# Two global attentions: heads in row and column groups of TensorE, scores computed twice, a pipeline of eight tasks

## The reference

```
gx = groupnorm(x)
xn = layernorm_channels(gx) * gamma1 + beta1
q, k, v = xn @ w_qkv + b_qkv                     # layer 0
o  = softmax(q k^T / 4) v                        # each head, 512 x 512
x1 = layernorm(o) * gamma2 + beta2, times w_out, + b_out + xn + x
q, k = [x1, emb] @ Wq, [x1, emb] @ Wk ; v = x1 @ Wv     # layer 1
x2 = softmax(q k^T / 4) v @ Wout + bout + x1
z  = layernorm(x2)
```

## Time and profile before

| | us |
|---|---|
| median of three runs | 8913.92 |
| lowest, highest | 8912.63, 8922.38 |
| the profiled execution's own time | 8909.57 |
| its span | 8907.7 |
| TensorE busy in it | 8128.0 (91%) |
| VectorE busy | 5894.3 (66%) |
| ScalarE busy | 2874.7 (32%) |
| GpSimd busy | 1260.6 (14%) |

### The profile page before, as it was taken

One profiled execution on the slowest core, in us unless ns is written; L12 is line 12 of the kernel. 1 busy time (PEld: TensorE's weight loads), 2 busy tenths in 40 slices (PEclk: granted clock), 3 DMA queues, 4 the chain that ended last, 5 costly groups with the idle time before them and its releaser, 6 DMA issues. The chain is left out here.

```text
span 8907.7 us, 387903 instructions
## 1 busy us (share of the span) xinstructions
PE 8128.0 (91%) x148885; PEld 5201.3 (58%) x148885; DVE 5894.3 (66%) x33160; ACT 2874.7 (32%) x10559; POOL 1260.6 (14%) x5288
## 2 busy tenths in 40 slices
PE   7777499999999999999999999999999999755886
PEld 3333166666666666666666666666666666544675
DVE  5665466666666666666666666666666666545997
ACT  4444122222222222222222222222222222235886
POOL 1000011111111111111111111111111111101001
PEclk9888599999999999999999999999999999867887
DMA  3110000000000000000000000000000000002332
GB/s 118 57 64 39 25 4 4 4 4 4 4 4 4 4 4 4 4 4 4 4 4 4 4 4 4 4 4 4 4 4 4 4 4 4 4 0 90 120 126 84
DMA packets 39897, 185.38 MB, mean 21 GB/s; under 512 B 7108, under 2 KB 20999, under 8 KB 27927
## 3 DMA queue, kind: packets, MB, share of 16 engines
q1 hardware_dynamic: 25638, 92.62, 2.7%
q0 software_dynamic: 12400, 67.68, 2.0%
HBM read 122.66 MB, written 37.62 MB: 18 GB/s over the span
## 5 line engine op out<-in xcount | busy, mean ns | idle before, releaser
L594 PEld LDWEIGHTS p<-H,W 128*128 128x128 f16 x130816 | 3572.9, 96 | 1940.8 <-DVE H L745 1918.8
L594 PE MATMUL p<-H,W 128*128 128x8 f16 x130816 | 3942.4, 167 | 74.7 <-DVE H L745 62.5
L606 PE MATMUL p<-W 128*128 128x500 f16 x12264 | 3261.0, 374 | 0.0
L745 DVE SCALAR_TENSOR_TENSOR H<-h,H 128x8 f16<-128x8 f32 x10220 | 1503.1, 163 | 279.7
L680 ACT ACTIVATE h<-u 128x8 f32<-128x8 f32 x4088 | 853.0, 209 | 2436.5 <-DVE u L765 2281.3
L675 ACT ACTIVATE h<-r 128x8 f32<-128x8 f32 x4088 | 851.7, 209 | 2405.0 <-DVE r L773 2220.5
L765 DVE TENSOR_REDUCE u<-p 128x8 f32<-128x24 f32 x6132 | 964.7, 175 | 804.2 <-PE p L594 804.2
L773 DVE TENSOR_REDUCE r<-p 128x8 f32<-128x24 f32 x4088 | 746.3, 183 | 1054.5 <-PE p L594 813.8
L740 DVE TENSOR_SCALAR H<-h 128x8 f16<-128x8 f32 x8176 | 1396.3, 171 | 41.0 <-issue 26.4
L606 PEld LDWEIGHTS p<-W 128*128 128x128 f16 x12264 | 884.1, 96 | 474.3 <-issue 9.4
L570 POOL TENSOR_TENSOR twice<-r 128x16 f32<-128x16 f32 x511 | 110.1, 215 | 2865.7 <-DVE r L773 2865.7
(11 more groups left out here) (328 smaller groups left out, 4939.2 us busy)
## 6 DMA issues: line engine op xcount, KB each, us to landing
e_W<-w_scaled SPq DMA_DIRECT2D x23, 2304.0 KB, 10.0
e_W<-w_scaled SPq DMA_DIRECT2D x23, 1152.0 KB, 5.1
raw<-in_spline POOLq DMA_DIRECT2D x24, 1024.0 KB, 6.8
w_scaled<-raw POOLq DMA_DIRECT2D x8, 2304.0 KB, 7.9
w_scaled<-raw POOLq DMA_DIRECT2D x8, 1152.0 KB, 10.0
raw<-in_base POOLq DMA_DIRECT2D x24, 128.0 KB, 6.6
raw_s<-in_scaler POOLq DMA_DIRECT2D x24, 128.0 KB, 7.0
rows_in<-zeros POOLq DMA_DIRECT2D x4, 768.0 KB, 16.3
```

Of the source, the lines that this page charges most:

```text
L594: ins = pe.matmul(out[:, m, 0:2 * B], W[:, q, k, P * m:P * m + P], H[:, k, :, :].rearrange("p q b -> p (q b)"), start=fresh[m], stop=(left ...
L606: pe.matmul(out[:, k, 3 * B:S], W2[:, 0, k, 0:P], W2[:, 1, k, 3 * B:S], start=True, stop=True, skip_group_check=True)
L745: sg.up(dve.scalar_tensor_tensor(out=Hq[:, :, 1, :], in0=mb(cols(h, q)), scalar=HSCALE, in1=Hq[:, :, 0, :], op0=ALU.mult, op1=ALU.subtract ...
```

## The change

The first stage is written out without a loop, as a pipeline of 8 tasks (`n`, layer `n // 4`, batch `n % 4`) in 10 rounds of 32 units. In round n, TensorE does `by_query` of task n, `by_key` and `weigh` of task n - 1, and `finish` of task n - 2, one piece after given units. The four batches' group norm and first layer norm go side by side ahead of it.

Queries and keys are kept in two versions (p = 0, 1), each with every second head; a group g of 32 rows then has one head's 16 channels and, in the other 16 rows, zeros and a one. `by_query` multiplies 32 rows of `qm` by 32 rows of `khat`, 128 queries by 512 keys, only for the maximum (`maximum`, VectorE, into `nmq`). `maxima_turned` transposes the negated maxima and `shift_queries` puts them in the free row of the queries (`qhat`), so that `by_key`, 128 keys by 512 queries, gives scores less their maximum; exp of it is at once what `weigh` wants, with no transposes. `weigh` writes 32 partitions of `pO` for each group: 16 of the output and one with the sum of the weights (a one in `vhat`). `finish` sorts sums and outputs by matmuls with `parts`; GpSimd raises the sums to the power -1, and VectorE multiplies the output by that. Variances are raised to the power -0.5 on GpSimd as well, in all layer norms of this stage. The group norm keeps Sqrt and `reciprocal`.

Of the experts' weights only those of expert 7 are made in this stage (VectorE in round 8). Those of experts 0 to 6 are made in the flow: SP loads and stores them, one expert an iteration, and VectorE scales half a part (128x128) in e = 1 of each of the steps 4 to 55.

```diff
+        pA, pC = [ps(f"pA{n}") for n in range(3)], [ps(f"pC{n}") for n in range(3)]
+        pO, pM = ps("pO"), ps("pM")
+        banks = pA + pC + [pO, pM]
...
+            raw.load(pool, a, NE - 1, sg, "ew_load")
+            for b in range(B):
+                sg.wait(pool, "n1_sd", b + 1)
+                sg.up(pool.tensor_tensor(sd[b][:], sd[b][:], halves[:], ALU.pow), "n1_rsd")
...
+            for n in range(TASKS):
+                sg.wait(pool, "s_copy", n + 1)
+                sg.wait(pool, "o_norm", n)
+                sg.up(pool.tensor_tensor(rr[:], ssb[:], ones_less[:], ALU.pow), "r_done")
+                if layer(n) == 0:
+                    sg.wait(pool, "n2_sd", batch(n) + 1)
+                    sg.up(pool.tensor_tensor(sd[0][:], sd[0][:], halves[:], ALU.pow), "n2_rsd")
+                if n == TASKS - 2:
+                    for b in range(2):
+                        sg.wait(pool, "n3_sd", b + 1)
+                        sg.up(pool.tensor_tensor(sd[b][:], sd[b][:], halves[:], ALU.pow), "n3_rsd")
+            for b in (2, 3):
+                sg.wait(pool, "n3_sd", b + 1)
+                sg.up(pool.tensor_tensor(sd[b][:], sd[b][:], halves[:], ALU.pow), "n3_rsd")
+            sg.wait(pool, "ew_scaled", 1)
+            raw.store(pool, t, NE - 1, sg, "ew_store")
+            sg.wait(pool, "ew_store", 16 * ExpertWeights.STORES)
...
+            def by_query(n, u):
+                p, j, g = u // 16, u // 4 % 4, u % 4
+                rows = slice(32 * g, 32 * g + 32)
+                if u == 0:
+                    sg.wait(pe, "khat", 2 * n + 2)
+                if n or u >= 3:
+                    sg.wait(pe, "a_max", UNITS * n + u - 2)
+                sg.up(pe.matmul(pA[(UNITS * n + u) % 3][:], qm[n % 2][p][rows, j * P:(j + 1) * P], khat[n % 3][p][rows, :],
+                                start=True, stop=True), "a_ps")
+            def by_key(n, u):
+                p, j, g = u // 16, u // 4 % 4, u % 4
+                rows = slice(32 * g, 32 * g + 32)
+                if u == 0:
+                    sg.wait(pe, "qhat", 2 * n + 2)
+                if n or u >= 3:
+                    sg.wait(pe, "prob", UNITS * n + u - 2)
+                sg.up(pe.matmul(pC[(UNITS * n + u) % 3][:], khat[n % 3][p][rows, j * P:(j + 1) * P], qhat[n % 2][p][rows, :],
+                                start=True, stop=True), "c_ps")
+            def weigh(n, k):
+                p, j = k // 4, k % 4
+                sg.wait(pe, "prob", UNITS * n + 4 * k + 4)
+                if k == 0:
+                    sg.wait(pe, "vhat", 2 * n + 2)
+                if j == 0:
+                    sg.wait(pe, "o_copy", 2 * n + p)
+                for g in range(GROUPS):
+                    ins = pe.matmul(pO[32 * g:32 * g + 32, :], vhat[n % 3][:, j, p, g, :], PT[(4 * k + g) % 8][:], start=(j == 0), stop=(j == 3))
+                sg.up(ins, "pv")
+            def maxima_turned(n):
+                sg.wait(pe, "a_max", UNITS * n + UNITS)
+                if n + 1 < TASKS:
+                    sg.wait(pe, "vhat", 2 * n + 4)
+                elif n >= 2:
+                    sg.wait(pe, "x2_done", batch(n - 2) + 1)
+                for j in range(QT):
+                    ins = pe.transpose(pM[:, j * P:(j + 1) * P], nmq[n % 2][:, j, :], t.ident[:])
+                sg.up(ins, "nm_ps")
...
+            def finish(n, u):
+                l, b = layer(n), batch(n)
+                if u == 2:
+                    sg.wait(pe, "o_copy", 2 * n + 2)
+                    sg.wait(pe, "qhat", min(2 * n + 4, 2 * TASKS))
+                    if n == TASKS - 1:
+                        sg.wait(pe, "x2_done", b)
+                    for p in range(2):
+                        ins = pe.matmul(pM[:], parts[:, p, :], osb[n % 2][p][:], start=(p == 0), stop=(p == 1))
+                    sg.up(ins, "sum_ps")
+                elif u == 6:
+                    sg.wait(pe, "s_copy", n + 1)
+                    for p in range(2):
+                        ins = pe.matmul(pM[:], parts[:, 2 + p, :], osb[n % 2][p][:], start=(p == 0), stop=(p == 1))
+                    sg.up(ins, "o_ps")
+                elif u == 10:
+                    sg.wait(pe, "o_norm", n + 1)
+                    if l == 0:
+                        sg.up(pe.matmul(pM[:], t.ones[:], oT[:], start=True, stop=True), "n2_mean")
+                    else:
+                        sg.up(pe.matmul(pM[:], w1["w1o"][:], oT[:], start=True, stop=True), "out_ps")
+                elif u == 14 and l == 0:
+                    sg.wait(pe, "n2_sq", b + 1)
+                    sg.up(pe.matmul(pM[:], t.ones[:], sq[0][:], start=True, stop=True), "n2_var")
+                elif u == 20 and l == 0:
+                    sg.wait(pe, "on", b + 1)
+                    sg.up(pe.matmul(pM[:], wo0[:], on[:], start=True, stop=True), "out_ps")
...
+            queries(0)
+            keys(0)
+            values(0)
+            for n in range(TASKS + 2):
+                for u in range(UNITS):
+                    if n >= 2:
+                        finish(n - 2, u)
+                    if n < TASKS:
+                        by_query(n, u)
+                    if 1 <= n <= TASKS:
+                        by_key(n - 1, u)
+                        if u % 4 == 3 and u > 4:
+                            weigh(n - 1, u // 4 - 1)
+                    if n + 1 < TASKS:
+                        if u == 23:
+                            queries(n + 1)
+                        elif u == 26:
+                            keys(n + 1)
+                        elif u == 29:
+                            values(n + 1)
+                    if n == TASKS and u in (3, 4):
+                        z_mean(u - 3, pA[u - 3])
+                    if n == TASKS and u in (11, 12):
+                        if u == 12:
+                            sg.wait(pe, "n3_cent", 2)
+                        z_var(u - 11, (pA[2], pA[0])[u - 11])
+                if 1 <= n <= TASKS:
+                    weigh(n - 1, 7)
+                if n < TASKS:
+                    maxima_turned(n)
...
+            def prob(n, u):
+                sg.wait(act, "c_ps", UNITS * n + u + 1)
+                sg.wait(act, "pv", 8 * n + u // 4 - 1)
+                sg.up(act.activation(PT[u % 8][:], pC[(UNITS * n + u) % 3][:], ACT.Exp), "prob")
+            def copy_o(n, p):
+                sg.wait(act, "pv", 8 * n + 4 * p + 4)
+                if n >= 2:
+                    sg.wait(act, "o_ps", n - 1)
+                sg.up(act.activation(osb[n % 2][p][:], pO[:], ACT.Copy), "o_copy")
...
+            for n in range(TASKS + 2):
+                for u in range(UNITS):
+                    if n >= 2:
+                        if u == 1:
+                            copy_o(n - 2, 1)
+                        elif u == 3:
+                            sg.wait(act, "sum_ps", n - 1)
+                            sg.wait(act, "r_done", n - 2)
+                            sg.up(act.activation(ssb[:], pM[:], ACT.Copy), "s_copy")
+                        elif u == 13 and layer(n - 2) == 0:
+                            sg.wait(act, "n2_cent", batch(n - 2) + 1)
+                            sg.up(act.activation(sq[0][:], xc[0][:], ACT.Square), "n2_sq")
+                        elif u == 16 and layer(n - 2) == 0:
+                            shifted_variance(act, sg, sd[0][:], pM[:], t.eps[:], "n2_var", batch(n - 2) + 1, "n2_sd")
+                    if 1 <= n <= TASKS:
+                        prob(n - 1, u)
+                        if u == 21:
+                            copy_o(n - 1, 0)
+                    if n + 1 < TASKS:
+                        if u in (24, 25):
+                            projected(n + 1, "qm", qm, u - 24)
+                        elif u in (27, 28):
+                            projected(n + 1, "khat", khat, u - 27)
...
+            def maximum(n, u):
+                p, j, g = u // 16, u // 4 % 4, u % 4
+                at = 32 * g + 16 * (1 - p)
+                sg.wait(dve, "a_ps", UNITS * n + u + 1)
+                if n >= 2 and u == 0:
+                    sg.wait(dve, "nm_ps", n - 1)
+                sg.up(dve.tensor_reduce(nmq[n % 2][:, j, at:at + 1], pA[(UNITS * n + u) % 3][:], AX.X, ALU.max, negate=True), "a_max")
+            def shift_queries(n, p):
+                sg.wait(dve, "nm_ps", n + 1)
+                if n >= 2:
+                    sg.wait(dve, "c_ps", UNITS * (n - 1))
+                sg.up(dve.scalar_tensor_tensor(out=qhat[n % 2][p][:], in0=pM[:], scalar=mask(1 - p), in1=qm[n % 2][p][:],
+                                               op0=ALU.mult, op1=ALU.add), "qhat")
...
+            def finish(n, u):
+                l, b = layer(n), batch(n)
+                if u == 8:
+                    sg.wait(dve, "o_ps", n + 1)
+                    sg.wait(dve, "r_done", n + 1)
+                    sg.up(dve.tensor_tensor(oT[:], pM[:], rr[:], ALU.mult), "o_norm")
+                elif u == 12 and l == 0:
+                    sg.wait(dve, "n2_mean", b + 1)
```

(65 more changed lines are left out.)

406 lines of the change are left out of this document (200 added, 206 removed).

## The result

| | before, us | after, us |
|---|---|---|
| median of three runs | 8913.92 | 10211.07 |
| profiled execution | 8909.57 | 10198.04 |
| its span | 8907.7 | 10196.2 |

The ratio is 1.1445, with a 95% interval of 1.1417 to 1.1472: 14% slower, where 3.4% faster was forecast. One of the three runs, 10521.59 us, is left out of the ratio as disturbed.

The account below looks back on a forecast made before the run. TensorE was taken to bound the flow and the first stage's dense part, with single-operation chains at layer borders. The first stage falls from 926 to 623 us, the flow costs 0: 8611 us, range 8370 to 8820 for 8 in 10.

Parts of the forecast that it names:

- The powers: GpSimd's 128x512 powers in the first stage: 3.4 us each, range 0.5 to 7, mostly hidden behind other work.
- Rival 3: GpSimd powers in the first stage take 15 us each: 118 us back, 8730 us; chance 0.06.
- the cover of the sums: Sum handed over at unit 3, result wanted at 10: at 2.1 us a unit, hides up to about 11 us.
- Overlap of groups: TensorE's score and weighing matmuls in the rounds: partial overlap of array groups, 58 us a round, four units in 7.3 us.
- rival 2: First stage: groups run fully side by side and TensorE ceases to be the bound, 557 us less, 8357 us; chance 0.20.
- the prediction's rule of three passes in four: Scores on TensorE: same-group passes can't overlap, so of four passes a unit three remain, 1.28 us.
- the prediction's own sign: Stated test of being wrong: a unit in the rounds isn't between 1.3 and 2.1 us.
- The clock: TensorE's granted clock in the rounds: expected at 1.0, the full level of 2.4 GHz.
- Rival 4: TensorE's clock falls to its lower level on 32-row or 32-column matmuls: 394 us more, 9308 us; chance 0.08.
- The forecast's stage: First stage summed as 40 + 24 + 490 + 42 + 27 = 623 us against 926, 303 us less.
- The flow: Added 128x128 VectorE operations fit where VectorE waits for TensorE: cost 0, or 116 us if the cover were gone.

Follow-up runs that it names:

- the kernel with all rows: Changed kernel with powers replaced by products of constant tiles, and both score matmuls of every unit on all 128 rows instead of 32: 8662.45 us, one run.
- without powers: Changed kernel with each of the 20 GpSimd powers replaced by a product of two constant tiles of the same size: 8608.03 us.
- the fastest kernel: Changed kernel with Sqrt on ScalarE and VectorE reciprocals for the powers, and keys' and values' projections later: 8556.72 us, ratio 0.96.

## Why the prediction was wrong

Term by term, as the prediction has them:

- *The powers.* This is the step that failed. It took 3.4 us for a power, with 0.5 to 7 for the range, and the measured one is 82.15. The upper bound was a GpSimd product of 16 elements stretched to 512, 7 us; but that product's 0.22 us is mostly its fixed part (a product of 512 takes 1.46, so an element some 2.5 ns, an estimate from the two), and it says nothing of a power. The sentence beside it, that nothing holds a power harder than a product from above, was right, and should have set the range. The nearest row in kind, the reciprocal on another engine, was no evidence for this engine.
- *Rival 3*, the long power, was the right mechanism with too small a size. Its formula, 4 x (p - 5) + 8 x (p - 11) + 4 x (p - 3.4), gives 1193 us for p = 82.15; it left out the four powers of the last norm, another 329. Together 1521, against VectorE's measured waits of 1581. Most of the rest is the cover of the sums: forecast 11 us with 2.1 us a unit, measured 82.15 - 610.4 / 8 = 5.9, as five units of 1.2 us have it.
- *Overlap of groups.* Forecast 7.3 us for four units at the full level, measured 4.81, nearer to rival 2. Eight passes of the weighing take 1.0 us and not 2.1; sixteen of the scores 3.81 and not 5.1. That the passes of one group alternate with the next didn't cost what the prediction's rule of three passes in four says: on average almost two passes run side by side (6.86 us of passes in 3.81). By the prediction's own sign it was wrong here too: a unit was to take 1.3 to 2.1 us and took 1.2. The change between matmuls on all rows and columns and the weighing's column groups, which rival 2 left without a price, is small in the kernel with all rows: a score matmul just behind the weighing takes 0.96 us to the start of the next, where 0.86 is usual (170.08, 171.04, 171.90).
- The Trainium skill's figure for four row tiles ("TensorE: Matmul & The Clock Gate", Part 3), 3.07 times, can't be compared with the scores, which alternate two on a group; the four column groups gained 3.43 / 1.0 = 3.4 times.
- *The clock.* Forecast at the full level; it is 0.78 without powers. Rival 4's fall of the clock is real, but it takes in part of the time only, and where it holds it has half the price: four units with their weighing were to take 4 x 3 + 5 = 17 us at the lower level and took 8.43, since the groups overlap there too.
- *The sum without powers.* The forecast's stage was 623 us, that without powers is 622.7, and the forecast 8611 us stands beside 8608. That is luck and no confirmation. From the starts of the first score and of the transposes of the maxima (42.82, 83.74, 553.58), the start took 43 us (forecast 40), round 0 41 (24; its clock was 0.50), rounds 1 to 7 together 470 (490), and the rest 69 (69). The rounds came near 70 only because the overlap was larger and the clock lower than forecast: round 1 took 76.7 us at a clock of 0.55, round 7, which has no projections, 48.7 at 0.93.
- *The flow.* Forecast 0, measured -2 us of 6571. The new operation stands where it was expected; VectorE's timeline, beside the earlier trace rows:

```profile
4612.47 0.17 DVE L969 SCALAR_TENSOR_TENSOR H<-h,H 128x8 f16<-128x8 f32 x1
4612.56 0.28 DVE L1057 TENSOR_TENSOR raw_f<-raw_f,raw_s_f 128x128 f32<-128x128 f32 x1
4613.09 0.47 DVE L995 TENSOR_REDUCE u<-p 128x8 f32<-128x24 f32 x3 [0.25 <-PE p L818]
```

It is 0.28 us long and VectorE still waits 0.25 us for TensorE after it.

## What to carry to other kernels

An operation that no row shows, on an engine where no row shows its kind, has no upper bound from the trace: the forecast then needs the question at what price the gain is gone (here 27 us a power: rival 3's formula set equal to the 304 us that the stage gained without powers), and a chance for it that doesn't lean on the price one hopes for. One small run that does the operation alone, in two sizes, on an idle engine would have answered it before any of the pipeline was written.

A rewrite that packs heads into row and column groups halves the dense part while the clock is at its full level (4.81 us for four units instead of 9.53), but look at the granted clock with it: count what TensorE does in each stretch, not only whether it is busy. With the powers undone and the projections moved, the rewrite is 4% faster than the kernel before.

Ask also which part of a rewrite brings the gain. Without powers the new kernel is 313 us faster than the one before; with all 128 rows in the scores, where no two scores overlap, it is still 254 us faster. So the row groups, on which the prediction spent most of its working, are worth 54 us by these two single runs; the rest comes with the pipeline of tasks, the transposes that are gone and the column groups, which no run tells apart.

## What the runs showed of the hardware

- A float32 power on GpSimd takes 160 ns for each element of the free axis, and as long on 16 partitions as on 128: 2.90, 20.78 and 82.17 us for 16, 128 and 512. A product of 512 takes 1.04 to 1.46 us.
- Float32 matmuls on different row or column groups run side by side: eight passes on four column groups start within 1.0 us at the full level, eight passes in single file within 3.43; sixteen passes, four on each of four row groups, start within 3.81 us instead of 6.86.
- TensorE, 98% busy with score matmuls on one group of 32 rows, had a mean granted clock of 0.54; the same number of matmuls with 128 rows, at 96% busy, had 0.98; and 32-row matmuls on four groups side by side ran from 400 to 480 us of the fastest kernel at 1.00.
